# Output projection head by head on 64-row matmuls, with the factor r applied on VectorE afterwards

## What is computed

```python
def tanh_norm(t):                       # per head and row, over its 64 numbers
    n = norm(t); return tanh(n) * (t / max(n, EPS))
# attention: 16 heads, 16 key numbers, 64 value numbers
attn = square(relu(l2norm(q) @ l2norm(k).T))
aggr = attn @ l2norm(v)
out  = tanh_norm(aggr) * tanh(silu(gates))
x    = x + concat_heads(out) @ Wout      # Wout: 1024 x 128
# experts: route each row to 4 of 16, then
g, u = x2 @ w_gate, x2 @ w_up            # per expert
y    = sum_e combine[e] * ((silu(g) * u) @ w_down) + shared
x    = x + y
```

## Time and profile before

| what | us |
|---|---|
| median of 3 runs | 668.57 (667.22 to 675.01) |
| the profiled execution | 669.18, of which the span from first to last instruction is 667.5 |
| TensorE busy | 647.6 |
| VectorE busy | 449.4 |
| GpSimd busy | 436.5 |
| ScalarE busy | 432.3 |

### The profile page before, as it was taken

How to read it: one execution, slowest core, us unless ns; L and a number is a source line. 1 busy time by engine, 2 the same in 40 slices (tenths; PEclk the granted TensorE clock), 3 DMA queues, 4 the chain that set the end, 5 groups by cost and what they waited for, 6 DMA issues and landing times.

```text
span 667.5 us, 15365 instructions
## 1 busy us (share of the span) xinstructions
PE 647.6 (97%) x5112; PEld 505.7 (76%) x5112; DVE 449.4 (67%) x1692; ACT 432.3 (65%) x1003; POOL 436.5 (65%) x443
## 2 busy tenths in 40 slices
PE   8799989999999999999999999999999999989998
PEld 6665657687877878787787878778787877767787
DVE  6656676685867668586767858676785856656665
ACT  5788775767566686756668675666867566645433
POOL 6667674867677576756757675676767576585532
PEclk9799999999999999999999999999999999999999
DMA  5049999694949869594986959497685939703000
GB/s 170 9 145 200 120 153 136 120 115 120 115 90 151 129 112 108 135 113 91 153 125 116 101 141 114 89 156 122 115 97 138 119 75 151 120 0 81 2 8 17
DMA packets 72557, 72.99 MB, mean 109 GB/s; under 512 B 9408, under 2 KB 70432, under 8 KB 70688
## 3 DMA queue, kind: packets, MB, share of 16 engines
q1 hardware_dynamic: 72480, 72.03, 67.4%
HBM read 53.95 MB, written 18.06 MB: 108 GB/s over the span
## 4 chain that ended last, share of the span: by engine, by line
PE 84%; DVE 5%; ACT 3%; DMA 3%; issue 3%; POOL 2%; SPq 0%; DVEq 0%; POOLq 0%; ACTq 0%
PE ps_a L725 17%; PE ps_f L531 12%; PE ps_f L532 9%; PE ps_f L533 9%; PE ps_f L638 9%; PE ps_f L611 8%; PE ps_s L685 7%; PE ps_f L583 3%; PE ps_f L604 3%; POOL p L459 2%; PE ps_f L588 1%; PE ps_f L620 1%; DMA c_rows<-ctr 1%; DMA cb<-c_rows 1%; DMA big<-in_L_attn_Wkv 1%
## 5 line engine op out<-in xcount | busy, mean ns | idle before, releaser
L459 POOL TENSOR_TENSOR p<-r 128x512 f32<-128x512 f32 x256 | 262.4, 1046 | 169.2 <-ACT r L766 103.2
L725 PE MATMUL ps_a<-p,v 128*64 128x256 f32 x1024 | 144.6, 394 | 7.2 <-DVE big L1189 3.7
L766 ACT ACTIVATE r<-ps_s 128x512 f32<-128x512 f32 x256 | 140.3, 610 | 13.5 <-PE ps_s L685 10.6
L1189 DVE TENSOR_TENSOR big<-ps_a,big 128x256 f32<-128x256 f32 x128 | 54.0, 422 | 74.0 <-ACT big L858 73.2
L725 PEld LDWEIGHTS ps_a<-p,v 128*64 128x64 f32 x1024 | 64.9, 136 | 46.5 <-DVE big L1189 5.8
L511 POOL TENSOR_TENSOR it<-it,cb 128x512 f32<-128x512 f32 x56 | 71.1, 1280 | 23.7 <-DMA cb<-c_rows 23.7
L810 ACT ACTIVATE big<-ps_f 128x512 f32<-128x512 f32 x64 | 38.2, 599 | 60.3 <-PE ps_f L533 60.2
L839 ACT ACTIVATE it<-ps_f 128x256 f32<-128x256 f32 x135 | 52.8, 391 | 32.0 <-PE ps_f L533 29.0
L1142 DVE TENSOR_TENSOR it<-ps_f,it 128x256 f32<-128x256 f32 x130 | 54.6, 420 | 24.2 <-ACT it L839 23.1
L479 POOL TENSOR_TENSOR v<-v,vs 128x512 f32<-128x512 f32 x64 | 67.0, 1057 | 1.6 <-DVE vs L1050 1.6
L685 PE MATMUL ps_s<-qkt 64*128 64x256 f32 x512 | 64.9, 331 | 0.0
(11 more groups left out here) (178 smaller groups left out, 1467.7 us busy)
## 6 DMA issues: line engine op xcount, KB each, us to landing
qk_rows<-qk_parts SPq DMA_DIRECT2D x15, 1024.0 KB, 4.4
qkt<-qk_rows SPq DMA_DIRECT2D x56, 256.0 KB, 10.3
qkt<-qk_rows SPq DMA_DIRECT2D x112, 128.0 KB, 9.5
cb<-c_rows SPq DMA_DIRECT2D x28, 512.0 KB, 5.7
x_in<-in_L_attn_tokens SPq DMA_DIRECT2D x16, 128.0 KB, 6.3
qkt<-qk_rows SPq DMA_DIRECT2D x32, 64.0 KB, 3.2
x_res<-in_L_attn_tokens SPq DMA_DIRECT2D x16, 128.0 KB, 8.9
out<-o_sb SPq DMA_DIRECT2D x16, 128.0 KB, 9.0
```

The source lines that it names most:

```text
L459: pool.tensor_tensor(p[h % 4][:], r[h % 2][:], r[h % 2][:], ALU.mult).then_inc(probs_done, 1)
L725: last = pe.matmul(ps_a[64 * e:64 * e + 64, 0:N], v[s % 3][:, t, h * DV:(h + 1) * DV], p[h % 4][:, t * N:(t + 1) * N], start=(t == 0), sto ...
L766: act.activation(r[h % 2][:], ps_s[h % 2][:], ACT.Relu).then_inc(relu_done, 1)
```

## The change

- `rT`, `rB`, `rt`, `split` of r, `scale_heads`, `residual_row` and the two jobs `y` go. r stays where it is computed, as `r_s`, one number for each row and head.
- Four double jobs `ya`/`yb` come in slots 2 to 5, each last in its slot and thus before the scores. `ya` issues nothing itself; `yb` j issues eight matmuls, for one half of the rows and four pairs of heads: the even head of a pair on array rows 0 to 63 into the bank of `ya`, the odd one on rows 64 to 127 into the bank of `yb`.
- `head_rows(j)` on VectorE adds these products, times `r_s`, one after the other to the residual row: eight `scalar_tensor_tensor` of 128x128, each waiting for the one before (`link_y`). The first four free the bank of `ya`, the other four that of `yb`. It stands ahead of the gated head in slots 3 to 6.
- Of nine gate/up products a step, chunks 0 to 3 go to GpSimd: ScalarE copies the up half to `up` (it shares the buffer of `qk_sq`), GpSimd multiplies two chunks at a time in slots 3 and 4.
- The jobs and VectorE's list are put in another order: `low_parts(1)` and the gate/up product 6 come behind `head_rows(3)` and `second_stats`, `normed_rows` moves ahead into slot 2, GpSimd's second root moves from slot 6 to slot 7.

```diff
     FILL = [
         [("F", "lg", 0), ("P", "v", 3), ("D", "y2", 0), ("N", "ones", 0)],
         [("N", "nT", 0), ("D", "y2", 1), ("P", "g", 0)],
-        [("F", "gu", 0), ("F", "gu", 1), ("P", "g", 1), ("F", "gu", 2)],
-        [("F", "gu", 3), ("F", "cD", 0), ("P", "g", 2), ("O", "rT", 0), ("F", "gu", 4)],
-        [("O", "rB", 0), ("O", "rB", 1), ("F", "gu", 5), ("O", "rB", 2), ("L", "xT", 0), ("O", "rB", 3), ("P", "g", 3)],
-        [("O", "y", 0), ("O", "y", 1), ("L", "qk", 0)],
-        [("F", "gu", 6), ("L", "qk", 1), ("L", "v", 0), ("F", "gu", 7)],
-        [("L", "v", 1), ("F", "gu", 8), ("O", "x2T", 0), ("L", "v", 2), SKIP, SKIP],
+        [("F", "gu", 0), ("F", "gu", 1), ("P", "g", 1), ("O", "ya", 0), ("O", "yb", 0)],
+        [("F", "gu", 2), ("F", "gu", 3), ("F", "cD", 0), ("P", "g", 2), ("O", "ya", 1), ("O", "yb", 1)],
+        [("F", "gu", 4), ("L", "xT", 0), ("F", "gu", 5), ("P", "g", 3), ("O", "ya", 2), ("O", "yb", 2)],
+        [("L", "qk", 0), ("L", "qk", 1), ("O", "ya", 3), ("O", "yb", 3)],
+        [("F", "gu", 6), ("L", "v", 0), ("L", "v", 1)],
+        [("F", "gu", 7), ("F", "gu", 8), ("L", "v", 2), ("O", "x2T", 0), SKIP],
     ]
...
+                    if "F" in on and at < B and k in (3, 4):
+                        j = k - 3
+                        pool.wait_ge(read["gu"], FC * (s - 2) + 2 * j + 2)
+                        part = it[:, 2 * j:2 * j + 2, :]
+                        pool.tensor_tensor(part, part, up[:, 2 * j:2 * j + 2, :], ALU.mult).then_inc(up_gated, 1)
...
-                    if k == 6 and "O" in on:
+                    if k == 7 and "O" in on:
                         pool.wait_ge(ch_n, 3 * s)
                         root(rstd2, var2, rstd2_ready)
...
+                elif kind == "ya":
+                    return
+                elif kind == "yb":
+                    t, half = divmod(j, 2)
+                    if j == 0:
+                        pe.wait_ge(aw_done, 8 * b + 8)
+                    for i in range(4):
+                        for e in range(2):
+                            rows = slice(64 * e, 64 * e + 64)
+                            last = pe.matmul(bank[(stage, "yb" if e else "ya", j)][:, i * D:(i + 1) * D],
+                                             heads3[b % 3][rows, 4 * half + i, tok[t]], wout[rows, 4 * half + i, :],
+                                             start=True, stop=True)
...
+                    if 4 <= b and b - 4 < B - 2:
+                        act.wait_ge(up_gated, 2 * (b - 4) + 2)
                     act.activation(qk_sq[:, j, :, :], whole, ACT.Square).then_inc(qk_squared, 1)
...
+                    if gated_by_two(b, j):
+                        if j == 0:
+                            wait(act, up_gated, 2 * b)
+                        act.activation(up[:, j, :], ps[:, N:2 * N], ACT.Copy).then_inc(read[kind], 1)
...
+                def head_rows(j):
+
+                    t, half = divmod(j, 2)
+                    if j == 0:
+                        dve.wait_ge(x_back[pq], (b - pq) * 8 + 16)
+                    dve.wait_ge(done["yb"], 4 * b + j + 1)
+                    row = x1[pq][:, t, :]
+                    for e in range(2):
+                        kind = "yb" if e else "ya"
+                        for i in range(4):
+                            h = 2 * (4 * half + i) + e
+                            so_far = x_res[pq][:, t, :] if (half, e, i) == (0, 0, 0) else row
+                            last = dve.scalar_tensor_tensor(out=row, in0=bank[("O", kind, j)][:, i * D:(i + 1) * D],
+                                                            scalar=r_s[:, t, h:h + 1], in1=so_far,
+                                                            op0=ALU.mult, op1=ALU.add)
+                            if i < 3:
+                                link_y(last)
+                        last.then_inc(read[kind], 1)
+                        dve.wait_ge(read[kind], 4 * b + j + 1)
...
                     if k == 6:
+                        if O:
+                            head_rows(3)
                         gated_heads(k)
+                        if O:
+                            second_stats()
+                        if L_on:
+                            low_parts(1, s + 2)
                         if F:
                             gate_up([6])
                         if L_on:
-                            low_parts(1, s + 2)
-                        if L_on:
                             sums(0, s + 2)
+                    if k == 7:
+                        gated_heads(k)
                         if O:
                             second_norm()
                         if F:
                             gate_up([7])
```

## The result

The kernel after takes 784.3 us (median of 5 runs, 783.2 to 789.0) where the kernel before takes 668.9 beside it: ratio 1.172, 95% interval 1.168 to 1.176. Slower, as forecast, but 39 us above the 745 forecast and 6 above the end of the range.

What follows compares the result with a forecast made beforehand. TensorE's work was taken as the bound: 36.8 us a step plus 7.2 of waits gives 44.0, 5.1 more than now. Twelve steps (+61) and the ends sum to 77.5 on 669.2; 745 us forecast, range 688 to 778.

Steps and rivals of the forecast that it cites:

- TensorE's side: Each step: head jobs of 0.90 us with products side by side; 36.8 us without waits, 2.1 less than before.
- Rival 4: Head jobs: 64-row fp32 products don't run side by side, four jobs take 7.2 us; 795 in all, chance 0.05.
- rivals 1, 2, 3 and 6: Link 0.325: 718, chance 0.17; link 0.265: 689, 0.07; only 2.1 us gain counts: 643, 0.04; waits partly overlap: 669, 0.04.
- The walk's waits: TensorE's waits in slots 3 to 7 of a step, 7.2 us together, 3.6 of them in slot 6; steps of 44.0.
- `var`: Slot 6, VectorE's chain ahead of `v` 0: priced at 0.64 us, ending with GpSimd's running product.
- A fall in each step: Rival 5: TensorE's clock falls in slot 6's hole, some 6.8 us at half pace; up to 790, chance 0.07.
- the ends: Outside steps 2 to 13: step 1 +4 us, steps 14 and 15 +3 each, the tail's norm 6.5 later.
- Even at 0.29 a link it would be 2.9: Slot 6, TensorE's wait before `v` 0: 3.6 us at the forecast price, 2.9 with cheaper links.
- the link's price: Each chained VectorE addition in `head_rows`: 0.325 to 0.38 us, taken as 0.38; eight links 3.04 us, 32 are 12.2.

Runs made afterwards that it cites:

- b2: The changed kernel with `low_parts(1)` ahead of `head_rows(3)` and even and odd heads summed in two alternating tiles: 727.0 us, ratio 1.086.
- a2: The changed kernel with 28 matmuls whose result nobody reads put on TensorE before `v` 0 in steps 1 to 13: 767.1 and 770.7 us, ratio 1.147.
- d3: The kernel before, with `v` 0 made to wait for six chained spare VectorE additions in steps 2 to 13: 744.2 us, ratio 1.110.
- c2: The changed kernel with only its tail reordered, `x2T` before the `y2` jobs and the second norm before the last scaling and output rows: 780.7 us, ratio 1.160.
- a3: The changed kernel with 24 of a step's 32 head additions left out, order unchanged: 731.6 us, ratio 1.091.
- a1: The changed kernel with `low_parts(1)` moved ahead of `head_rows(3)` in slot 6: 733.9 us, ratio 1.097.
- d1: The changed kernel with `low_parts(1)` moved ahead of the second statistics only: 761.1 us, ratio 1.133.
- b1: The changed kernel with `low_parts(1)` ahead of `head_rows(3)` and GpSimd's second root between its squares 14 and 15: 709.6 us, ratio 1.061.
- b4: The changed kernel with the edits of a1, b1, b2 and c2 together: 697.0 us, ratio 1.041.
- b3: The changed kernel with `low_parts(1)` ahead of `head_rows(3)` and 24 of 32 head additions left out: 722.5 us, ratio 1.081.
- d2: The changed kernel with the edits of b4 and c1, and `x2T` one place later in the order of the banks: 696.6 us, ratio 1.038.
- c1: The changed kernel with `var` made by a `tensor_tensor` against a constant tile instead of a `tensor_scalar`: 779.7 us, ratio 1.164.

## Why the prediction was right in kind and too low in size

**TensorE's side was right.** Chained links at 0.38 us, VectorE at 33.9 and 32.8 us in the two steps shown (33.8 forecast), GpSimd 29.05 (29.1), ScalarE 27.7 (27.6). From the start of a head job to that of the scores behind it 0.91 us pass (341.31 to 342.22 in step 7; forecast 0.90, and 1.8 if the pairs of products ran one after the other), so they run side by side. Rival 4 is out, and so are rivals 1, 2, 3 and 6: b2 shows that 0.26 a link needs additions that don't wait for each other, and then too the time is 727, not 689.

**The walk's waits were right in place and nearly in size.** Every wait that it named is in the list: slots 3 to 5 within 0.1 us, slot 6 first, `x2T` next. With the clock held up (a2) a step is 44.5 for the forecast 44.0. That it comes so near is in part luck: `var` took 0.17 there for the walk's 0.64, and without it the walk's other terms are 0.9 us a step too low, most of it in slot 7 (6.25 for 5.8) and slot 6 (7.1 for 6.9 at that `var`).

**Step that failed: the clock was left to a rival.** "A fall in each step ... adds 3.4 us or less: up to 790" got a chance of 0.07, and that is what came. Steps 2 to 13 at a2's 44.5 would be +66 on before; they are +91. Of the 25 between, 9 are `var`'s and some 17 the clock's (estimate, a2 above). The 43 us by which the profiled execution missed 746 are then some 17 of clock, 12.5 at the ends, 3 of `var` (0.92 on average for 0.64) and some 11 of other waits in the steps, with 0.7 back at the start. Without the clock's 17 the time would be 767, inside the range; a2's two runs, 767 and 771, lie there too, with `var`'s luck in them. The rival's own size, 3.4 us a step or less, was an upper bound: it came to 1.4. The row that should have raised the chance was there: after a stretch with 1.4 of 2 us idle the clock had fallen in the kernel before, and the walk put a hole of 3.6 us into every step. The forecast summed the waits and kept a clock of 1.00, which in the kernel before hung on there being no such hole: d3 puts one in, and the clock falls in all twelve steps.

**Term mis-sized: `var`.** It was priced at 0.64 us "since it starts at 350.67 and ends with GpSimd's running product". That is right as a mechanism, but the duration depends on where in GpSimd's work it falls. In eight steps it met the start of a product and took 1.30; in the others, some ten nanoseconds earlier against it, 0.17. At equal falls of the clock that is the difference between steps of 46.5 and 45.4 us.

**Term mis-sized: the ends**, 29.0 us for 16.5. Of the 12.5 missed 7 are the tail. Three head jobs there wait 1.4 to 1.7 us each for the rows before them, and the clock is at half in part of it, and the tail's list puts `x2T` behind two `y2` jobs, 7 us together, which the walk left out: it moved the norm by the links' 12.2 less the scalings and took TensorE to be free. c2 gives 2.2 us of it back. What the clock has of the rest wasn't separated.

**The claim "Even at 0.29 a link it would be 2.9" held and was the important one**: a3 shows 2.2 to 2.8 us with links all but gone. I had it as an aside; it should have moved the weight from the link's price to the order. I named the link's price as the likeliest error, and it was exact.

What the 115 us consist of, as far as runs separate it (a sum of overlapping edits, so each figure is for its own run against its neighbour): slot 6's order with what hangs on it 50 (a1), of which the statistics and `var` 23 (d1), and the clock behind that hole some 17 (estimate, a2), which overlap; the root's place 24 (b1); the two sums and the tail's order together 13 (b4 against b1). The remaining 28 stay in b4.

## What to carry to other kernels

Before work is added to an engine that has room, walk each job that shares a rotating buffer and ask what now stands ahead of its reader: the place of one 0.69 us operation was worth 50 us here, and leaving out 24 of 32 additions 53. A hole in TensorE's stream is to be priced with the clock behind it: those of 3.1 to 4.2 us here cost some 1.4 us more a step, those of 4.3 in d3 some 1.8 (both estimates, above). A hole filled with idle products (a2) shows that share, once it is checked that nothing else differs between the two traces; here `var` did. When several jobs are late together, a single wait removed hands its time to the next, and the longer hole can bring the clock down: b2 and b3 gained nearly nothing in the steps while the root was late, and d2 nothing while the gate/up product was.

## What the runs showed of the hardware

- A VectorE operation on two numbers per partition, out of and into SBUF, lasts 0.17 or 1.30 us depending on how it meets GpSimd's 128x512 product, in two different forms. A product that starts up to 12 ns behind it holds it up to its own end, one that starts 18 ns or more behind doesn't, and in between both are seen.
- A VectorE addition of 128 columns out of PSUM starts 0.38 us after the one whose result it takes, and 0.26 after one that it doesn't depend on. The Trainium skill (VectorE: DVE Perf Modes, section on the DRAIN you can't avoid) has the semaphore cost nothing extra between copies; for these operations a wait for the neighbour costs 0.12 us.
- What a fall of the clock costs depends on where in the step it lies: in c1's profiled execution steps of 47.65, 45.34 and 44.45 us follow each other at equal work and equal `var`, with 6.8 us at half pace in slot 0, 6.8 in slots 6 and 7, and 3.4 there. The last costs nothing (a2's step without a fall is 44.47), for `x2T` would have waited anyway. c1's runs lay between 776 and 787 us, those of the kernel before within 1%. So small edits such as c1 and c2 are read from their rows, not from totals.
